# A decoder layer on one core: six row scatters in flight, expert weights halved at other places, one pair's transposes in plain order

## What is computed

```
x = x + attn(norm(x))            strided attention, 16 heads, ternary weights
x = x + cross(norm(x), ctx)      64 keys per sequence, the top 54 kept
x = x + ffn(norm(x))             shared expert + 4 of 16 routed experts
```

## Time and profile before

| | |
|---|---|
| median of 3 runs | 720.62 us (719.58 to 725.29) |
| profiled execution | 723.11 us |
| its span, first to last instruction | 721.3 us |
| PE / DVE / ACT / POOL busy | 615.3 / 555.6 / 414.8 / 489.2 us |
| granted TensorE clock, mean | 0.942 |
| attention / cross / expert phase | about 0 to 184 / 184 to 415 / 415 to 721 us |

### The profile page before, as it was taken

One profiled execution on the slowest core, in us unless ns is written; L12 is line 12 of the kernel. 1 busy time (PEld: TensorE's weight loads), 2 busy tenths in 40 slices (PEclk: granted clock), 3 DMA queues, 4 the chain that ended last, 5 costly groups with the idle time before them and its releaser, 6 DMA issues. The chain is left out here.

```text
span 721.3 us, 15858 instructions
## 1 busy us (share of the span) xinstructions
PE 615.3 (85%) x4034; PEld 537.4 (75%) x4034; DVE 555.6 (77%) x1745; ACT 414.8 (58%) x1140; POOL 489.2 (68%) x373
## 2 busy tenths in 40 slices
PE   0787889987778999999772079999999999999993
PEld 0676778866456776676541069999999999999993
DVE  3987957885667888878648379888888888888883
ACT  1695567533345656574325078666666666666662
POOL 2499999981003655577777617877777776878776
PEclk9998999999988999999896579999999999999997
DMA  8930010031433577743446337888888887878874
GB/s 283 299 119 30 15 45 30 30 124 37 135 143 117 193 251 272 265 145 137 148 149 220 137 108 121 146 141 144 137 148 138 139 144 118 153 136 154 148 110 58
DMA packets 77093, 100.37 MB, mean 139 GB/s; under 512 B 9744, under 2 KB 70304, under 8 KB 76448
## 3 DMA queue, kind: packets, MB, share of 16 engines
q0 software_dynamic: 26736, 37.64, 28.3%
q1 hardware_dynamic: 48096, 59.64, 27.2%
q10 hardware_dynamic: 2176, 2.10, 0.9%
HBM read 50.97 MB, written 52.95 MB: 144 GB/s over the span
## 5 line engine op out<-in xcount | busy, mean ns | idle before, releaser
L1749 POOL DMA_INDIRECT out_dram<-yw,xg x143 | 222.0, 1553 | 83.5 <-issue 59.6
L1372 POOL DMA_INDIRECT xs_scratch<-rows,slot x128 | 126.7, 990 | 99.2 <-issue 73.0
L1632 PE MATMUL cbank<-w,stc_hi 112*128 (+1 forms) x572 | 109.5, 284 | 0.4 <-DVE stc_hi L1714 0.4
L1632 PE MATMUL cbank<-w_hi,xtc_hi 128*128 x286 | 105.3, 368 | 0.1
L1632 PEld LDWEIGHTS cbank<-w,stc_hi 112*128 112x128 f32 (+1 forms) x572 | 94.3, 189 | 1.6 <-issue 1.0
L1639 ACT ACTIVATE xtc_hi<-cbank 128x256 fp32r<-128x256 f32 x143 | 55.0, 385 | 67.3 <-PE cbank L1621 66.8
L1632 PE MATMUL cbank<-w_hi,xtc_lo 128*128 x286 | 93.1, 325 | 0.0
L1632 PE MATMUL cbank<-w,xtc_hi 128*128 x286 | 92.2, 322 | 0.0
L1621 PE MATMUL cbank<-identb,xg 128*128 128x128 f32 x286 | 55.3, 275 | 30.6 <-DMA xg<-xs_scratch 30.6
L1735 DVE TENSOR_SCALAR yw<-cbank,xg 128x256 f32<-128x256 f32 x143 | 69.2, 484 | 3.4 <-PE cbank L1632 0.6
L1686 DVE TENSOR_TENSOR hh<-cbank,h 128x176 f32<-128x176 f32 x143 | 48.9, 342 | 24.8 <-ACT h L1680 22.7
(11 more groups left out here) (240 smaller groups left out, 1546.3 us busy)
## 6 DMA issues: line engine op xcount, KB each, us to landing
xg<-xs_scratch SPq DMA_DIRECT2D x143, 144.0 KB, 2.6
w<-w13r_dram SPq DMA_DIRECT2D x8, 704.0 KB, 6.4
w_hi<-ctx_t_dram SPq DMA_DIRECT2D x8, 512.0 KB, 3.5
x_scratch<-x_all SPq DMA_DIRECT2D x16, 256.0 KB, 2.1
w_hi<-x_scratch SPq DMA_DIRECT2D x8, 512.0 KB, 4.6
out_dram<-w SPq DMA_DIRECT2D x16, 256.0 KB
w<-w2r_dram SPq DMA_DIRECT2D x4, 1024.0 KB, 8.9
x_all<-x_dram SPq DMA_DIRECT2D x12, 256.0 KB, 9.6
```

The lines of the kernel that those rows point to most:

```text
L1372: nc.gpsimd.indirect_dma_start(t["xs"], bass.IndirectOffsetOnAxis(ap=slot[:, n % 2, k:k + 1].bitcast(U32), axis=0), rows[:, n % NROW, k // ...
L1632: last = nc.tensor.matmul(out, stationary, moving, start=j == 0, stop=j == len(pairs) - 1)
L1749: nc.gpsimd.indirect_dma_start(t["out"], bass.IndirectOffsetOnAxis(ap=xg[:, p, ID:ID + 1].bitcast(U32), axis=0), yw[:, p % YB, :], None, c ...
```

## The change

Three edits. The number of scatters in flight, and of lanes, goes from 3 to 6. The two splits are cut into pieces and moved in the lists of the cross phase: on ACT experts 0 to 9 stand behind `xhC` in turn 9 and 10 to 15 behind `g1r_` in turn 10; on DVE 0 to 4 and 5 to 9 stand before and behind `hs_` in turn 9, 10 and 11 before `hs_` in turn 10, and 12 to 15 at the end. In the attention phase the order of the halves is turned round for pair 15 alone and no longer for pair 14.

```diff
-FLY = 3
+FLY = 6
...
         def out_t0(eng, j):
-            out_t(eng, j, 1 if j in LATE else 0)
+            out_t(eng, j, 1 if j == LATE[-1] else 0)
 
         def out_t1(eng, j):
-            out_t(eng, j, 0 if j in LATE else 1)
+            out_t(eng, j, 0 if j == LATE[-1] else 1)
...
-            v=[(1, negs), (3, shares), (3, spread), (1, tops), (1, masks), (3, hsr_), (-1, stA), (3, hs_), (1, x2_), (1, stC),
-               (-1, root, NG + 2), (2, choose), (3, table), (3, xf_(0)), (3, xf_(1)), (3, split_lo(range(NE)))],
-            s=[(0, xhA), (1, expo), (1, at_second_ev), (3, g1r_), (2, xhC), (1, bp_ev), (1, p_t_ev), (3, g1_), (2, t_c_ev), (0, t_a_ev),
-               (2, th_), (0, at_later_ev), (3, split_hi(range(NE)))],
+            v=[(1, negs), (3, shares), (3, spread), (1, tops), (1, masks), (3, hsr_), (-1, stA), (2, split_lo(range(0, 5))),
+               (3, split_lo(range(10, 12))), (3, hs_), (2, split_lo(range(5, 10))), (1, x2_), (1, stC), (-1, root, NG + 2), (2, choose),
+               (3, table), (3, xf_(0)), (3, xf_(1)), (3, split_lo(range(12, NE)))],
+            s=[(0, xhA), (1, expo), (1, at_second_ev), (3, g1r_), (3, split_hi(range(10, NE))), (2, xhC),
+               (2, split_hi(range(0, 10))), (1, bp_ev), (1, p_t_ev), (3, g1_), (2, t_c_ev), (0, t_a_ev),
+               (2, th_), (0, at_later_ev)],
```

## The result

The changed kernel took 716.1 us (median of 4 runs, 710.91 to 717.31) beside 722.01 us for the kernel before (4 runs, 719.58 to 725.29): ratio 0.9911, 95% interval [0.9882, 0.9939]. So 5.9 us were gained where 12.2 were forecast. The profiled execution took 717.31 us with a span of 715.2 (before: 723.11 and 721.3).

What follows compares the result with a forecast made beforehand. POOL's chain of 128 scatters was taken to set the cross phase's end, with attention's end a chain of its own. Gains 8.8 + 0 + 3.4 = 12.2 us from the 720.62 median left 708.4; predicted 709, range 703 to 717.

Steps and rivals of the forecast that it cites:

- part 2: Cross phase: moving most ACT copies and DVE subtractions earlier was forecast to gain 0 us by itself.
- the same 3.3 us are paid, no more and no less: Cross phase: POOL's scatters slowed beside DVE's subtractions would lose 3.3 us in the new place as in the old.
- far from a full block: Cross phase: scatters of 1.31 against 0.96 us beside DVE's subtractions were read as much less than full blocking.
- The third rival: Cross phase: each DVE subtraction stops scatters for its whole length, 14.1 instead of 3.3 us, 719 us; chance 0.07.
- Part 1: Cross phase: six scatters under way instead of three remove nearly all POOL's waits for landings; gain 8.8 us.
- rivals 1 and 4: Cross phase: scatters' waits are want of transfer rate (713 or 717 us, chance 0.13); POOL's issue gets longer (736 us, 0.04).
- Part 3: End of attention: plain order of halves for pair 14 brings the barrier forward; gain 3.4 us.
- the part of it that is the clock's: End of attention: without PE's long idle stretch its clock stays full, saving 1.2 us on 16 transposes and 0.4 on projection.

## Why the prediction was wrong

The step that failed is the price in part 2: "the same 3.3 us are paid, no more and no less". It was read from the place where DVE's subtractions then stood, and taken to be a property of the two engines together. In the new place one scatter per batch is held until the batch ends: 9.3 us in the changed kernel, and 8.2 between its time and that of the same kernel without early halves. The reading under the price failed with it. The 1.31 us was taken for "far from a full block", and it was a full block by one subtraction, of which only the last half microsecond was left. (The 3.3 itself was 2.8: the eight scatters of the window were all that stood beside subtractions.) The third rival, blocking for the whole of the subtractions, had chance 0.07 and was the one that came about, for the three early batches. It was priced at 14.1 us against 9.3 measured, mainly because the four subtractions at the end of the list stayed mild (0.7 us together); it gave 719. The Trainium skill (SBUF — State Buffer, section Who interferes with whom) says that the shared port is locked, that whichever comes first keeps it, and that the other is fully blocked. By this case's rows that fits the scatters of 1.30 us, which wait for one instruction of VectorE. Those of 4.61 and 8.62 us go beyond it, as they wait for five and ten instructions in a row, and coming first didn't help: the scatter of 2.55 us is recorded as starting 0.04 us before its batch, and the one of 2.81 us 0.30 before. Yet one that starts 0.03 us before a batch (363.83, halves early alone) took 0.96.

When the block is full and when it is mild is not settled. PE's clock isn't it: it was granted at 1.00 in a full one (the changed kernel, 354.00 to 363.80 above), and in the window of the mild batch of the kernel with the halves early alone:

```profile
363.90:368.00 4.10, 2.68 (x11) 1.38 (x11) 4.06 (x6) 2.00 (x5) 3.48 (x3) 1.00 0.33 110
```
ScalarE's copies aren't it: in the changed kernel they ended at 365.64, and at 369.42 the block is full all the same. The number under way isn't it, as both kinds stand in one trace with three. Nor is it that the scatter meets the first subtraction of a batch, as the expectation for ten in a row has it: in the changed kernel the scatter at 384.91 starts 0.38 us behind the first of four (384.53) and is held by that one alone, while those at 354.57 and 359.49, 0.30 and 0.61 us behind the first of five, are held by all five.

Part 1, six under way, was right in mechanism and in size: 8.8 us forecast, 10.1 measured alone, with an interval of 5.5 to 11.9. The waits of 26.1 us went, the chain is POOL's from quad 5 on, and no rate limit or longer issue showed (rivals 1 and 4 fall, on this sort of chip).

Part 3 came out right: 3.4 forecast, 3.5 read between POOL's product and the barrier. But the part of it that is the clock's rests on a reading that doesn't hold everywhere. The clock was said to fall after the idle stretch before the 16 transposes. With six under way alone, which has the old order, PE waits the same 2.57 us and the clock stays at 1.00:

```profile
167.70 1.94 PE L461 MATMUL ps_t<-ident,pv 128*128 128x128 f32 x16 [2.57 <-DVE pv L442]
```

There the stretch from POOL's product to the last normalisation took 16.8 us, against 17.7 before and 14.2 with plain order. So about 2.6 us come from the order and 0.9 from a clock that falls in some executions of the old order and not in others. The difference of the two kernels with six under way, 711.86 and 705.27, is larger, 6.6 us. In the profiled executions the rest goes with where PE's clock falls: 214 to 230 us was granted 1.00 in the 705 us kernel, 0.79 in the 712 us one, and the wait before quad 1 was 1.52 against 4.65 us. That this comes from the order wasn't shown, as the order alone was only timed on another sort of chip.

That part 2 is worth nothing by itself failed with the price: with the halves early alone, 4.5 us were lost. Its reason held on the 722 sort. PE's first expert work stands 7.0 to 7.4 us behind the end of the last scatter in each of these kernels. It held narrowly where the halves stay at the end: with six under way DVE's last subtraction ends at 393.35, 0.8 us behind the last scatter (392.59), whose rows have yet to land. On the chip with 779 us, in the two traces with copies and subtractions all at the end, PE's work stood 4.9 us behind DVE's last one; by that distance (an estimate) DVE has 1.4 us to spare here, as PE started at 399.62.

The sum with the measured terms: -10.1 - 6.6 + 8.2 = -8.5, against -8.5 measured on that chip (713.51 and 721.97) and -5.9 on the chip of the result. The terms are differences of those four kernels, so they add up by their making; that both chips agree within their intervals is the only test in it.

The versions with five or eight under way, plain order and the halves where they had been beat both kernels: 705.16 and 704.82 us, 0.978 and 0.977, as does six (705.27, 0.980). Between these three nothing is shown, since single executions of one of them lie up to 5 us apart (704.71 to 710.14 with eight).

## What to carry to other kernels

When an engine's work is moved into a stretch where another engine is the bound, the price of the two beside each other must be taken for the new stretch, and a slowdown of a third in the old one is no bound. Look at what the slowed instruction's end follows, since a short wait can be a full block by a short instruction; ask what a full block for the whole batch would cost, and give it more than a token chance. The busy time of an instruction that only issues transfers is no work; where its mean rises, look for the few long ones and for who ends just before they do. And time a version on more than one chip if a part of it depends on waits between engines: here six under way with the plain order gave 0.98 on one chip and 1.02 on another.

## What was not expected of the hardware

An indirect transfer's issue on POOL, ordinarily 0.96 us, can be held for 8.62 us by ten VectorE subtractions of two SBUF operands in a row, and is done 0.83 to 0.84 us after them. The issues that take 1.30 us end as far behind a single subtraction. ScalarE's copies of the same tiles cost it nothing. And chips of one kind can differ by 8% in this kernel (722 against 779 and 785 us), and nearly all of it lies in the cross phase: from the first to the last scatter-add of the expert phase it is 284.8 to 284.9 us on either sort (424.3 to 709.2 in the changed kernel, 495.1 to 780.0 with six under way on the chip with 779).
